# Storing the edge counts of six source groups in both orientations, in a four-layer graph network on Trainium2

## What is computed

```python
edge_index = jnp.stack([src, dst])
h = jnp.maximum(_layernorm(x, axis=-1), 0.0)
x = x + _L0_gnn_ref(h, src, dst, edge_weight, L0_gnn_weight, L0_gnn_bias)  # out[src] += w * h[dst], then a 48x48 product
h = jnp.maximum(_layernorm(x, axis=-1), 0.0)
x = x + _L1_gnn_ref(h, edge_attr_48, src, dst, L1_gnn_eps)                 # out[dst] += relu(h[src] + edge_attr)
h = jnp.maximum(_layernorm(x, axis=-1), 0.0)
x = x + _L2_gnn_ref(src, dst, h)                                          # twice: out[src] += norm * h[dst]
h = jnp.maximum(_layernorm(x, axis=-1), 0.0)
x = x + _L3_gnn_ref(h, edge_index, 12500)                                 # once, the other way: out[dst] += norm * h[src]
```

## Time and profile before

| what | value |
|---|---|
| median of 3 runs | 11184.18 us |
| lowest and highest | 11174.97 and 11187.02 us |
| the profiled execution | 11290.17 us |
| its span, first to last instruction | 11287.9 us |
| granted PE clock over the span | 0.733 of full speed |
| first stage, up to the last cast to `stg` | to about 6906 us |
| last propagation on PE | 10262.5 to 11222.1 us |
| instructions | 257760 |
| DMA packets and bytes | 2133134 packets, 2069.27 MB |

### The profile page before, as it was taken

The page is one execution under the profiler, slowest core; times in us unless marked ns, Lnnn a source line. Parts: engine busy times, 40 slices in busy tenths (PEclk is TensorE's granted clock), DMA queues, the critical chain, the costliest instruction groups (busy, mean ns, idle before and its releaser), DMA issues.

```text
span 11287.9 us, 257760 instructions
## 1 busy us (share of the span) xinstructions
PE 6251.7 (55%) x98007; PEld 5362.1 (48%) x98008; DVE 5001.7 (44%) x7173; ACT 2140.3 (19%) x5352; POOL 4093.2 (36%) x4193
## 2 busy tenths in 40 slices
PE   2444444444444444444444444877883996995775
PEld 1333333333333333333333333777773996994765
DVE  4444445444444444444444545999994001002000
ACT  1222222222222222222222222222220000000000
POOL 1444444444444444444444441777771000000000
PEclk5666666666665666666665666999997998998998
DMA  6454445454454444544444542888885776778998
GB/s 191 152 164 155 154 151 165 152 158 155 146 163 148 150 155 155 161 153 154 155 151 143 169 147 66 301 294 293 295 295 171 257 247 195 260 244 148 183 182 157
DMA packets 2133134, 2069.27 MB, mean 183 GB/s; under 512 B 1327507, under 2 KB 1761971, under 8 KB 2132355
## 3 DMA queue, kind: packets, MB, share of 16 engines
q1 hardware_dynamic: 1784138, 1461.21, 45.6%
q10 hardware_dynamic: 248592, 443.28, 11.2%
q0 software_dynamic: 100000, 158.60, 4.4%
HBM read 1257.86 MB, written 634.57 MB: 168 GB/s over the span
## 4 chain that ended last, share of the span: by engine, by line
PE 28%; issue 23%; another core or an unknown queue 17%; DVE 14%; SPq 8%; DMA 4%; ACT 3%; DVEq 1%; POOL 1%; ACTq 0%; POOLq 0%
PE pG L1849 8%; SPq L2174 7%; PE pG L1703 4%; PE pT L1746 3%; ACT stg L1953 3%; PE pT L1849 2%; DVE msum L1580 2%; DVE doh L1401 2%; PE pG L1714 2%; PE pG L1712 2%; PE pR L1849 2%; DMA cA<-stg 2%; DVE val L1414 1%; PE pG L1691 1%
## 5 line engine op out<-in xcount | busy, mean ns | idle before, releaser
L1242 POOL DMA_INDIRECT recB<-rec,qpos x3125 | 3044.8, 974 | 3794.7 <-issue 3794.7
L1746 PE MATMUL pT<-soh,doh 128*128 128x128 bf16 x10600 | 1316.3, 263 | 2020.9 <-ACT stg L1953 1425.4
L1953 ACT CAST stg<-pT 128x512 fp8e4<-128x512 f32 x2650 | 1482.1, 587 | 4405.2 <-remote 3244.8
L1746 PEld LDWEIGHTS pT<-soh,doh 128*128 128x128 bf16 x10600 | 776.7, 115 | 2150.1 <-ACT stg L1953 1557.5
L1703 PE MATMUL pG<-hw,dT 128*128 128x48 bf16 x9420 | 615.6, 211 | 1095.2 <-issue 1092.8
L1849 PE MATMUL pG<-xw,cl 128*128 128x144 bf16 x13780 | 1051.4, 228 | 289.9 <-DMA cl<-cA 262.7
L1419 DVE TENSOR_TENSOR rec<-pG,wN 128x480 f32<-128x480 f32 x314 | 206.0, 656 | 2228.4 <-PE pG L1703 2181.3
L1703 PEld LDWEIGHTS pG<-hw,dT 128*128 128x128 bf16 x9420 | 455.5, 114 | 1339.5 <-issue 1334.0
L1849 PEld LDWEIGHTS pG<-xw,cl 128*128 128x128 fp8e4 x13780 | 914.8, 99 | 291.7 <-issue 291.7
L1401 DVE TENSOR_TENSOR soh<-smd,pG 128x1280 bf16<-128x1280 bf16 x530 | 431.6, 814 | 1056.5 <-remote 1031.9
L1825 PE MATMUL pG<-mpl,doh 128*128 128x144 bf16 x10388 | 778.9, 229 | 200.3 <-POOL mpl L1263 193.0
(11 more groups left out here) (200 smaller groups left out, 10929.7 us busy)
## 6 DMA issues: line engine op xcount, KB each, us to landing
cl<-cA SPq DMA_DIRECT2D x100, 2880.0 KB, 11.0
recB<-zt ACTq DMA_DIRECT2D x108, 2425.5 KB
brec<-recB SPq DMA_DIRECT2D x477, 495.0 KB
erec<-recB SPq DMA_DIRECT2D x477, 495.0 KB, 3.9
cA<-stg ACTq DMA_DIRECT2D x530, 320.0 KB
srowB<-srD SPq DMA_DIRECT2D x477, 320.0 KB, 4.1
drow<-dlD SPq DMA_DIRECT2D x157, 640.0 KB, 6.4
rec<-in_edge_attr_dram SPq DMA_DIRECT2D x156, 480.0 KB
```

What stands on the lines that cost most here:

```text
L1242: p.indirect_dma_start(recF, bass.IndirectOffsetOnAxis(ap=qpos[:, s, c:c + 1], axis=0), rec[:, s, c, :], None, bounds_check=NK * 128 * NB ...
L1746: ins = t.matmul(B8[6 + (g * 5 + e) % 2][:, h * 256 + b * 128:h * 256 + b * 128 + 128], doh[:, o, 2 * e + b, h * 128:(h + 1) * 128], soh[: ...
L1953: a.copy(stg[:, o, :, e * 256:(e + 1) * 256], B8[6 + (g * 5 + e) % 2][:, :].rearrange("p (h x) -> p h x", h=2), saturate=False).then_inc(e ...
```

## The change

Groups 0 to 5 (`GT = 6`) get their counts stored a second time, in a new DRAM tensor `cB`, with the sources on the partitions.

In the first stage PE adds to each of the five steps of such a group two matmuls with one-hot operands exchanged. Each has 256 columns, and together they fill bank `B8[7]`. The ordinary counts of these groups then always use `B8[6]`. ACT adds one cast for each step, into a new tile `stgT`, and one store of 320 KB for each group. `counts(K, g)` numbers the casts now, since a group has ten or five of them. The tables that spread the groups over the slots are as before.

In the last propagation groups 0 to 5 are loaded plainly from `cB` into a new ring `tb` of three buffers (six loads of 1600 KB in an iteration, 100 matmuls each). Groups 6 to 9 are transposed as before (19 transposes in an iteration). `TURNS` mixes the two kinds: one plain load, then three or four transposes, and so on. The matmuls per iteration stay 980. The plain part multiplies with `xpc`, which is in SBUF already, and `xq` keeps 19 of its 49 parts. SP issues the first three plain loads and seven transposes before it waits for `t3`.

The core of the diff:

```diff
+GT = 6
+        cB = dram("cB", (GT, NK, 128, GB * 128), BF16)
+        stgT = pha("stgT", [128, 2, GB * 256], F8)
-        xq = Placer(nc, phc.off)("xq", [128, 49, 2, 3 * D], BF16)
+        xq = Placer(nc, phc.off)("xq", [128, 49 - 5 * GT, 2, 3 * D], BF16)
+        tb = phs("tb", [128, 3, 5, GB * 128], BF16)
+        TURNS = [(k, 0) for k in range(GT)]
+        for q in range(49 - 5 * GT):
+            TURNS.insert(1 + (q * GT // (49 - 5 * GT)) + q, (q, 1))
+        NTU = len(TURNS)
+        CS = JG * 5 + GT * 5
+        def counts(K, g):
+            return K * CS + g * 5 + min(g, GT) * 5
...
 PE, bucket:
-                    reached(t, e_cv, c * 5 + (e - 1))
+                    n = e * (2 if g < GT else 1)
+                    reached(t, e_cv, counts(K, g) + (n - 1))
                     for b in range(2):
                         for h in range(2):
-                            ins = t.matmul(B8[6 + (g * 5 + e) % 2][:, h * 256 + b * 128:h * 256 + b * 128 + 128],
+                            ins = t.matmul(B8[6 + (counts(0, g) + n) % 2][:, h * 256 + b * 128:h * 256 + b * 128 + 128],
                                            doh[:, o, 2 * e + b, h * 128:(h + 1) * 128], soh[:, o, 2 * e + b, :],
                                            start=True, stop=True)
                     ins.then_inc(e_ca, 1)
+                    if g < GT:
+                        reached(t, e_cv, counts(K, g) + n)
+                        for b in range(2):
+                            ins = t.matmul(B8[7][:, b * 256:(b + 1) * 256], soh[:, o, 2 * e + b, :], doh[:, o, 2 * e + b, :],
+                                           start=True, stop=True)
+                        ins.then_inc(e_ca, 1)
...
 ACT, bucket:
                 held(a, s_cs[o], K * 80 + g // 2 * 16)
+                if g < GT:
+                    held(a, s_ct[o], K * (GT * 8) + g // 2 * 16)
...
+                    if g < GT:
+                        hold(a, e_ca, counts(K, g) + (n + 2))
+                        a.copy(stgT[:, o, e * 512:(e + 1) * 512], B8[7][:, :], saturate=False).then_inc(e_cv, 1)
...
+                if g < GT:
+                    a.dma_start(cB[g, bass.ds(K, 1)].rearrange("k p c -> p (k c)"), stgTB[:, o, :]).then_inc(s_ct[o], 16)
...
 SP, last propagation:
+                        if kind == 0:
+                            sp.dma_start(tb[:, q % 3, 0:nk, :], cB[q, bass.ds(i * 5, nk)].rearrange("k p c -> p k c")
+                                         ).then_inc(l_tb[q % 3], 16)
+                        else:
+                            g = q + 5 * GT
+                            sp.dma_start_transpose(
+                                ct[:, q % 7, 0:nk * 256].rearrange("p (o r) -> p o r", o=1),
+                                cA[g // 5, bass.ds(i * 5, nk), :, :, g % 5 * 128:g % 5 * 128 + 128]
...
+                sp.wait_ge(y_rd, 2 * JG * 6)
+                load_turned(0, 5, TURNS[:ahead], True)
                 sp.wait_ge(e_qn, qn["t3"])
```

More of the change, by code:

```diff
@@ L1135, in build @@
         s_cs = [sem(f"s_cs{k}") for k in range(2)]
+        s_ct = [sem(f"s_ct{k}") for k in range(2)]
         s_sr = sem("s_sr")
@@ L1144, in again, with turned_free, turned_uses @@
             return [next(spare) for _ in range(n)]
+        TURNS = [(k, 0) for k in range(GT)]
+        for q in range(49 - 5 * GT):
+            TURNS.insert(1 + (q * GT // (49 - 5 * GT)) + q, (q, 1))
+        NTU = len(TURNS)
+        def turned_free(j, kind):
+            ring = (3, 7)[kind]
+            mine = [n for n, x in enumerate(TURNS) if x[1] == kind and x[0] % ring == j % ring]
+            at = [n for n, x in enumerate(TURNS) if x == (j, kind)][0]
+            before = [n for n in mine if n < at]
+            return before[-1] if before else mine[-1] - NTU
+        def turned_uses(j, kind):
+            ring = (3, 7)[kind]
+            return len([x for x in TURNS if x[1] == kind and x[0] % ring == j % ring])
         t_tp, t_cp, t_mm = again(3)
@@ L1150, in build @@
         s_ht, l_xw, y_rd, y_ev, y_ad = again(5)
[L1151 removed]
+        l_c, l_t, l_tb = again(3), again(7), again(3)
         z_rd, z_ev = again(2)
@@ L1451, in columns @@
                 v.wait_ge(e_sm, c + 1)
-                reached(v, e_ca, c * 5 - 5)
+                if not isinstance(K, int) or c > 0:
+                    reached(v, e_ca, counts(K, g - 1) if g else counts(K - 1, JG - 1))
                 one_hots(soh[:, o, :, :], smd[:, r, :, 0, :], GB, 128, ioA)
```

74 lines of the change are left out of this document (43 added, 31 removed).

## The result

The kernel after takes 12054.6 us (median of 4 runs, 12039.6 to 12060.5), the kernel before 11185.6 us beside it (4 runs, 11175.0 to 11223.7). The ratio is 1.077, with an interval of 1.074 to 1.080. The change makes the kernel 7.7% slower. That is the forecast's sign, but 435 us above its value.

A forecast was written before the change was run, and what follows sets the result against it. POOL's indirect-DMA bursts and the gaps between them pace the first stage; the DMA engines bound the last propagation. 11290.2 + 655 + 18 - 233 = 11730 profiled, times 0.9906: 11620 us; own range 11480 to 11900, 80% range 11250 to 12100.

The forecast's parts named there:

- case without a gain: Rival: in the last propagation plain loads and transposes disturb each other, iterations stay at 89 us; median 11850, chance 0.04.
- gap before slot 1's burst: First stage, POOL's idle time before its second burst in a chunk: unchanged at 16 us.
- groups 1 and 2 (gap of slot 2): First stage, extra casts lengthen the gap before slot 2's burst: +4.5 us for group 1, +2.9 for group 2.
- groups 4 and 5 (gap of slot 0): First stage, extra casts lengthen the gap before slot 0's burst: +5.2 us a chunk, between +2.6 and +7.3.
- The slow stretch: First stage: while POOL issues indirect DMAs, PE crawls, its signals arrive late; some 25 us, about three casts pass.
- Groups 0 and 3 at nothing: First stage: their extra 2.9 us of casts lie beside the burst's first 4 us, costing nothing on the path.
- The stores: First stage, six more stores of 320 KB a chunk: nothing, or up to 2 us a chunk if late.
- fetched anew in each chunk: Rival: PE's loop code is fetched at each turn, 11.5 us more a chunk, 12210 us in all; chance 0.11.
- The last propagation: Plain loads replace 30 transposes an iteration: 735 us against 959.9, a gain of 225, bounds 152 to 266.
- The tail and the read-back: After the last burst, six doubled groups' casts cost 18 us; a shorter read-back of xq gains 8 us.
- The scaling: Whole kernel: profiled sum times 0.9906, before's median over its profiled execution, turning 11730 into 11620 us.

The follow-up runs named there:

- e12: The kernel after with only groups 1, 2, 4 and 5 doubled and ACT's loop set into three blocks of 128 instructions: ratio 1.041 to before.
- e4: The kernel before with ACT's loop padded by fulfilled waits to the length and place it has in the kernel after: ratio 1.062 to before.
- e2: The kernel after without the exchanged matmuls and second casts, its six extra stores kept: ratio 1.011 to before.
- e5: e2 with 60 more instructions (fulfilled waits) once ahead of ACT's loop: ratio 0.969 to before, on a chip without the slow stretch.
- e3: The kernel after with 128 more instructions (fulfilled waits) once ahead of ACT's loop: ratio 1.078 to before.
- e1: The first stage of the kernel after with the last propagation of the kernel before: ratio 1.100 to before.
- e7: The kernel after with only groups 1 and 4 doubled, ACT's loop set into three blocks: ratio 0.993 to before, without the slow stretch.
- e8: The kernel after with only groups 2 and 5 doubled, ACT's loop set into three blocks: ratio 0.992 to before, without the slow stretch.
- e9: The kernel after with only groups 1 and 5 doubled, ACT's loop set into three blocks: ratio 0.991 to before, without the slow stretch.
- e11: The kernel after, unchanged, run again on a chip without the slow stretch: ratio 0.996 to before.

## Why the prediction was right, and where it was off

The sign and the place of the loss were right on the chips where before takes 11200 us. The size was not: 12055 lies in the 80% range (11250 to 12100), near its end, but outside the forecast's own range of 11480 to 11900, and a chunk grew by 19.2 us where that range allowed 17. The wide range was drawn for a case without a gain, and that it holds a case with an unpriced cost instead is luck. Step by step, in us a chunk, once with all gaps and once with the kernel before taken without its five long ones:

| term | forecast | measured | without the five | from |
|---|---|---|---|---|
| gap before slot 1's burst | 0 | -0.4 | -0.4 | after |
| groups 1 and 2 (gap of slot 2) | 7.4 | 5.7 | 5.7 | e12 |
| group 0 | 0 | 1.9 | 1.9 | after less e12 |
| groups 4 and 5 (gap of slot 0) | 5.2 | 4.4 | 5.5 | e12 |
| turn of ACT's loop | none | 4.9 | 6.0 | e4 |
| the rest of slot 0's gap: group 3, stores | 0 | 2.6 | 1.5 | what is left of 11.9 or 13.0 |
| sum | 12.6 | 19.1 | 20.2 | 147.2 - 128.0 = 19.2 |

**The slow stretch as the price.** Right, and the reason why the sign was right. Of its two halves, that PE crawls is borne out, while that ACT only waits for late signals is not: ACT crawls too (e4). The stretch also came on some chips only, which the prediction couldn't see from one trace: it says "past 3 us after the burst's end" would make it wrong, and never asks whether the stretch is there at all.

**Groups 1 and 2, 4 and 5.** Right in kind. Groups 1 and 2 came out 1.7 us lower in e12, and groups 4 and 5 within 0.8 us on either count. The gap of slot 2 in after (+7.6) hits the forecast's 7.4 only because group 0's cost, which was left out, makes up for what groups 1 and 2 fall short. That the two agree to 0.2 us is luck.

**Groups 0 and 3 at nothing.** This step failed. The prediction says that their casts "eat the head start that groups 1 and 4 have now", and then costs that at zero. The sentence before says that their extra casts lie beside the burst's first 4 us; the last two of either group don't, they are caught by the stretch. For group 0 it is 1.9 us. For group 3 it is at most the rest of 1.5 to 2.6, in which the stores may have a part. That group 3 has a part I take from the casts (eight left over in after, four in e12), since no run has it alone on a chip with the stretch.

**The stores.** Costed at nothing up to 2 us. Slot 0's gap grew by 6.3 in e2 and by 4.9 in e4, with nearly the same stall at the turn. The 1.4 us between them are within these bounds and over the 0.5 us by which two traces differ. They are likely the six stores, but the two kernels also differ in where their code lies, so this isn't shown.

**The code.** The rival "fetched anew in each chunk" happened, but on ACT and not on PE, to which the prediction tied it. Its sum for PE (11.5 us a chunk) had no place in the result, and its size on ACT was 4.9 to 6.0. This is the term that the sum lacked. The prediction even names ACT's buffer as the nearer one, by the Trainium skill's "Runtime: NRT & Kernel Launch", section "Instruction fetch mechanics", and doesn't cost it. That page gives most engines room for 512 instructions; here bodies of 306 and 388 were fetched anew all the same, so the measurement decides. What fits all runs is the number of blocks of 128 instructions that the loop touches. A body of 306 was fetched anew in one place (e2) and stayed in another (e5), one of 352 stayed (e12), and one of 388 was fetched in both places tried (after, e3).

**The last propagation.** Forecast 735 us, measured 704.5, so 255 won instead of 225 and inside the bounds of 152 to 266. The iteration, 69 against 67.6, makes 13 of the 30 us; the rest is in iterations 0 and 10, which took 55 and 41 us instead of 64 and 50. Against 19 transposes at 1.82 us, the six plain loads got at most 67.6 - 34.6 = 33 us, 5.5 each, between the bounds of 4.7 and 6.1. The figure of the Trainium skill that spoke against a gain ("DMA: Bandwidth & Descriptors", section "Latency and other measured facts": 261 GB/s for a transpose) isn't reached here: e1 moves them at 180 GB/s at a full share, and taking 30 of 49 away won 250 us.

**The tail and the read-back.** Forecast +18 for the tail and -8 for the read-back of `xq`, 10 in all. From the last burst to the first matmul of the last propagation it is 33 us more. The tail is the mis-sized part: the last cast to `stg` comes 94.9 us after POOL's last DMA begins, and 65.2 before, 30 us more. The read-back did get shorter, from 13.4 to 6.5 us.

**The scaling.** The sum was multiplied by 0.9906, the median over the profiled execution. That step failed. The profiled execution of before (11290) was longer than any timed one of it, while in after and in e1, e2 and e12 the profiled span lies within 0.1% of the median (12058.2 and 12054.6; 12363.6 and 12357.2; 11363.0 and 11360.6; 11665.5 and 11655.1). What was taken for the cost of profiling was in the main the scatter of one execution, 60 us of it in the five long chunks that the prediction itself had seen. The step is worth 110 us.

Together: the first stage up to the last burst lost 992 us where 655 were forecast (+337), the tail with the read-back 33 instead of 10 (+23), the last propagation won 255 instead of 225 (-30), and the scaling took off 110 where after's profiled span lies 4 above the median (+106). That is the 435 us, but for rounding. The largest single step that failed is the code of ACT's loop, at nothing in the sum and 255 us by e4's gap (4.9 x 52).

## What to carry to other kernels

Before adding work to an engine's loop, count its instructions and look at the instruction queue's packets: when they scale with the number of iterations, the loop is fetched anew each time, here at 4.9 us x 52 = 255 us or more, as much as the whole gain of the change, and where the loop begins can decide it. A cost that hides beside other work still moves what comes after it on the same engine, so cost the neighbour's lost head start too. Look for outliers in the trace of the kernel before, too: five long chunks moved every difference in one gap here by 1.2 us. And before a few per cent are trusted, time both kernels on more than one chip: the bound itself may be another there.

## What the runs showed of the hardware

- The kernel before, unchanged, took 11183 to 11234 us in three sets of runs and 8774 and 8775 us in two; the four sets of the experiments were each on another chip. The work is the same; what differs is whether ACT and PE get on while POOL issues its indirect DMAs. With the stretch a chunk of the kernel before takes 128 us; without it a chunk takes 79 in e5, e7, e8 and e9. What makes a chip one or the other is open. Five sets of runs can't tell the chip itself from something that differs with the time.
- In such a stretch fulfilled waits on ACT took about 0.7 us (851 of the 5400 added waits in e4 lie between 0.6 and 0.8 us), outside 0.077 from one to the next. PE's weight loads and matmuls of `pick` came at the same steps: 1439 steps of 0.65 to 0.78 us in before, 472 to 1402 in after and in e1 to e4 and e12, and none in e5 to e11, on the chips without it.
- ACT's instructions come in packets of 8192 bytes, about one for 130 instructions. Loops of 280 to 352 instructions, all but the first set into three blocks of 128, ran without a fetch (40 to 55 packets in the whole run). One of 306 in another place and those of 388 paid 4.4 to 5.3 us at each turn and took five packets in each iteration (282 to 301), the last on chips of both kinds. The blocks are the reading, the packets and times are what was measured.
- Plain loads of 1600 KB and transposes of 320 KB on one queue, in turns, kept to what each was estimated at alone: 67.6 us an iteration, at 237 GB/s and a full DMA share, with PE at 94%.
